# Router products of 64 columns instead of 8 in the prologue, and 64 filling matmuls instead of 32 before the first slot

## The chip, the cores and the metric

The kernel runs on one core of a Trainium2 chip. The metric is the device time of one launch in microseconds, the median of several runs; lower is better.

## What is computed

A macaron block on x of 4 batches × 1024 tokens × 128 features, all float32:

```python
x = x + 0.5 * ffn(layernorm(x))      # top-1 mixture of 8 experts, 128 -> 512 -> 128, relu
x = x + attn(layernorm(x))           # 16 heads of 8, decayed linear attention in chunks of 128
x = x + 0.5 * ffn(layernorm(x))      # the same weights again
# inside ffn
logits = xf @ Wr.T + br              # Wr is 8 x 128
expert_idx = argmax(logits, axis=-1)
h = relu(einsum('td,efd->etf', xf, W1) + b1[:, None, :])
y = einsum('etf,edf->etd', h, W2) + b2[:, None, :]
out = y[expert_idx, arange(tokens)]
```

## The kernel before

Tokens are cut into 32 tiles of 128; four of them (the same chunk of each batch) make a step, and there are 8 steps. Five engines run their own instruction streams, written out by hand, with semaphores between them.

Each FFN pass computes only the chosen expert. The tokens of a group (group 0 is steps 0 to 4, group 1 steps 5 to 7) are sorted by expert into slots of 128 rows that each belong to one expert: 27 slots for group 0 and 19 for group 1. GpSimd gathers a slot's rows (L396) from a copy of the normalised rows in DRAM. TensorE transposes them (L1208), ScalarE copies the transpose to SBUF (L545), TensorE makes the four up products (L1216, 8 instructions), ScalarE and VectorE apply bias and relu (L560 and L924), TensorE makes the down product (L1226, 8 instructions), VectorE adds the bias (L937) and the result is stored to y_d. The second half of one slot's up products waits for L924 of the slot before. TensorE issues the transpose of slot G+1 first, then up of G, then down of G-1. In the first pass a table of extra work, by turn, sits between slots on VectorE: the rest of layer norm (turns 0 to 2) and the routing of group 1 (turns 3 to 13: L780 to L791 is turn 3). GpSimd then fetches the results back (L410).

The prologue runs before the first slot. On TensorE, in this order:

- `keep_warm_by_columns(WARM0)`: matmuls whose result nobody reads, with 32 columns of weights and 128 columns streamed (L1166).
- Nine rounds. Round r transposes step r (L1170, 4 instructions), and then multiplies the transposed step r-1 by the router weights (`route_product`, L1176): 4 products, which are 8 matmul instructions with a weight load each, 8 columns streamed. After the transposes of round 3 and its product comes one product for the sum of the router weights (L1364). In round 6 `route_counts(0)` (L1183, L1184) waits for VectorE's one-hot matrix of group 0.
- The gate and bias products (L1367, L1369), and `invert(0)` (L1192), whose result is the list of tokens by slot.
- `keep_warm_by_columns(WARM1)` again, then the slots.

ScalarE copies each transposed step to SBUF (L537). VectorE takes layer-norm statistics (L702), then scales the logits once the products of steps 0 to 4 are done (L789, L791), finds the best expert and the one-hot matrix (up to L814), counts and places tokens (L820 to L873), writes the experts of the slots (L903) and, after the inversion, the list of tokens (L884, token_in) that the first gather waits for.

```python
for i in range(count):
    for c in range(0, P, 32):
        mm(bank[3][c:c + 32, 0:P], ident[:, 0:32], const_sb[:, 0:P], start=True, stop=True)
```

`const_sb` begins with the identity; `wr_sb` holds the router weights, 8 columns. The products of group 0 go to bank 4, 8 columns for each tile, 160 in all, and those of group 1 to bank 6, 96 in all.

Of the kernel before, what the change touches and what calls it, by code (L numbers as in the profile page):

```python
# [15 lines left out]
P = 128  # L16
BATCH, SEQ, D = 4, 1024, 128
STEPS = SEQ // P
TOKEN_TILES = BATCH * STEPS
EXPERTS, FF = 8, 512  # L20
# [8 lines left out]
def list_units():  # L29
    units, start = [], 0  # L30
    for layer, split in enumerate(SPLIT):
        first = 0
        for steps in split:
            tiles = steps * BATCH
            units.append(Unit(layer, first, tiles, tiles + EXPERTS - 1, start))
            first += tiles
            start += tiles + EXPERTS - 1
    return units


UNIT = list_units()
# [31 lines left out]
CONST_W = _at  # L73
# [12 lines left out]
def wait(eng, sem, value):  # L86
    if value > 0:
        eng.wait_ge(sem, value)
# [15 lines left out]
def build(nc, x, w1t, bias, w2t, wrt, br, wqkv, wg1t, wg2, wo, gamma, beta, decay, const, out):  # L104
    with ExitStack() as ctx:
        def sb(name, shape, dt=F32):
            return ctx.enter_context(nc.sbuf_tensor(name, shape, dt))

        def pb(name, shape=(P, 512)):
            return ctx.enter_context(nc.psum_tensor(name, list(shape), F32))  # L110

        def sem(name):
            return ctx.enter_context(nc.semaphore(name))
# [15 lines left out]
        hT_a, hT_b = ([sb(f"hT_{h}{i}", [P, 2 * P]) for i in range(2)] for h in "ab")  # L129

        decay_sb = sb("decay_sb", [P, HEADS * P])
        const_sb = sb("const_sb", [P, CONST_W])
        wr_sb = sb("wr_sb", [P, EXPERTS])
        br_sb = sb("br_sb", [P, EXPERTS])
        wr_sum = sb("wr_sum", [P, EXPERTS])
        wqkv_sb = sb("wqkv_sb", [P, 3 * D])
# [10 lines left out]
        rnT = [sb(f"rnT{i}", [P, BATCH * P]) for i in range(2)]  # L147
# [60 lines left out]
        bank = [pb(f"bank{i}") for i in range(8)]  # L208
# [4 lines left out]
        def cst(name, rows_=P):  # L213
            a, w = CONST[name]
            return const_sb[0:rows_, a:a + w]
# [15 lines left out]
        wr_loaded, br_loaded, wg_loaded, attn_w_loaded = sem("wr_loaded"), sem("br_loaded"), sem("wg_loaded"), sem("attn_w_loaded")  # L231
# [6 lines left out]
        wr_summed, wr_sum_copied = sem("wr_summed"), sem("wr_sum_copied")  # L238
# [30 lines left out]
        table_loaded = sem("table_loaded")  # L269
        halved, ends_known = sem("halved"), sem("ends_known")  # L270

        WARM0, WARM1 = 3, 4
        LANE_PARTS = 4
        assert SPLIT[0] == (5, 3)

# [10 lines left out]
        router_bank = [bank[4], bank[6]]  # L286
# [231 lines left out]
        @block.scalar  # L518
        def _(act):
            act.dma_start(const_sb[:, 0:EARLY_W], const[:, 0:EARLY_W]).then_inc(ident_loaded, 16)  # L520
            act.dma_start(wr_sb[:, :], wrt).then_inc(wr_loaded, 16)
            act.dma_start(br_sb[:, :], br.partition_broadcast(P)).then_inc(br_loaded, 16)

            act.wait_ge(ident_loaded, 16)
# [158 lines left out]
            for i in range(2 * SPLIT[0][1]):  # L683
                r, lo = SPLIT[0][0] + i // 2, i % 2 * 2
# [468 lines left out]
        def _(pe):  # L1153
            mm = nc.tensor.matmul
# [13 lines left out]
            def transpose4(dst, src, done):  # L1168
                for b in range(BATCH):
                    last = nc.tensor.transpose(dst[:, b * P:(b + 1) * P], src(b), ident)  # L1170
                last.then_inc(done, 1)

            def route_product(r, par, dst, at):
                pe.wait_ge(rnT_copied, r + 1)
                for b in range(BATCH):
                    last = mm(dst[:, at + b * EXPERTS:at + (b + 1) * EXPERTS], rnT[par][:, b * P:(b + 1) * P], wr_sb[:, :],  # L1176
                              start=True, stop=True)
                last.then_inc(logits_ready, 1)

            def route_counts(u):  # L1180
                pe.wait_ge(onehot_ready[u], 1)
                n = UNIT[u].tiles * EXPERTS
                mm(counts_bank[:, 0:n], upper_bf[:, :], onehot_bf[:, 0:n], start=True, stop=True)  # L1183
                mm(counts_bank[:, n:2 * n], ones_bf[:, :], onehot_bf[:, 0:n], start=True, stop=True).then_inc(counts_ready[u], 1)  # L1184
# [133 lines left out]
            def attention(k):  # L1318
                cur, nxt = step(k), step(k + 1)
                has_cur, has_nxt = 0 <= k < STEPS, 0 <= k + 1 < STEPS  # L1320
                for h in range(PAIRS):
                    if has_cur:
                        state_product(cur, h)
                    if h == 0 and 0 <= k - 2 < STEPS:
                        out_product(step(k - 2))
                    if has_nxt:
                        if h == 0 and k >= 0:
                            norm_transpose(nxt)
                        if 1 <= h <= BATCH:
                            project(nxt, h - 1)  # L1330
                        if h == BATCH + 2:
                            q_transpose(nxt)
                    if has_cur and h == BATCH + 1:
                        gate_product(cur)
                    if 0 <= k - 3 and h == BATCH + 2:
                        route_transpose(step(k - 3))
                if has_cur:
                    inter_product(cur)
                    if k + 1 < STEPS:
                        carry_product(cur)  # L1340
                if 0 <= k - 3:
                    s = step(k - 3)
                    route_product(STEPS + s.n, s.par, bank[4], 0)
                if 0 <= k - 1 < STEPS:
                    out_transpose(step(k - 1))
# [4 lines left out]
            for r in range(STEPS + 1):  # L1350

                if r < STEPS:
                    pe.wait_ge(x_loaded[r], 16)
                    wait(pe, rnT_copied, r - 1)
                    transpose4(bank[r % 2], lambda b: x_of(r * BATCH + b), rnT_ready)
                if r == SPLIT[0][0] + 1:
                    pe.wait_ge(bf_ready, 1)
                    route_counts(0)
                if r >= 1:
                    g = 0 if r - 1 < SPLIT[0][0] else 1  # L1360
                    route_product(r - 1, (r - 1) % 2, router_bank[g], (r - 1 - UNIT[g].first // BATCH) * BATCH * EXPERTS)
                if r == 3:
                    pe.wait_ge(const_loaded, 16)
                    mm(bank[7][:, 0:EXPERTS], cst("ones"), wr_sb[:, :], start=True, stop=True).then_inc(wr_summed, 1)  # L1364
            pe.wait_ge(wg_loaded, 16 * 2)
            pe.wait_ge(b1_loaded, 16)
            mm(bank[3][:, 0:D], wg1_sb, wg2_sb, start=True, stop=True)  # L1367
            for f in range(FB):
                last = nc.tensor.transpose(bank[3][:, D + f * EXPERTS:D + (f + 1) * EXPERTS], b1_rows[:, f * P:(f + 1) * P],  # L1369
                                           ident[0:EXPERTS, 0:EXPERTS])  # L1370
# [11 lines left out]
            for k in TURNS:  # L1382
                attention(k)
                if k == ROUTE_TURN:
# [3 lines left out]
                    invert(2)  # L1388
            pe.wait_ge(qS_done, STEPS * PAIRS)
            route = lambda s: route_product(STEPS + s, s % 2, bank[4], 0)  # L1390
            expert_pass(1, {
                0: lambda: out_transpose(step(7)), 1: lambda: route(5), 2: lambda: out_product(step(7)),
# [65 lines left out]
```

## Time and profile before

| | |
|---|---|
| median of 3 runs | 430.17 us (429.95 to 430.38) |
| profiled execution | 426.96 us, its span 424.9 us |
| mean granted TensorE clock | 0.909 of full |
| TensorE busy | 358.1 us, 84% of the span |
| VectorE, ScalarE, GpSimd busy | 68%, 45%, 67% |
| x to SBUF | 8 loads of 256 KB |

TensorE's clock has two levels, 2.4 GHz (1.00 in the profile) and 1.2 GHz (0.50). Times in the rows are microseconds from the span's start. A matmul's own duration includes its way through the pipeline; what a run of matmuls costs is the distance from one group to the next, which the chain of waits shows.

### The profile page before, as it was taken

To read this page: it belongs to the slowest core of one execution; us is meant where nothing else is said; L and a number is where in the kernel's file an instruction comes from. 1 tells how busy PE (TensorE), PEld (TensorE's weight loads), DVE (VectorE), ACT (ScalarE), POOL (GpSimd) and SP (SyncE) were. 2 spreads that over 40 slices of the span, in tenths; PEclk is the share of its full clock that TensorE was granted. 3 is DMA by queue.
4 is the path that set the end of the run, shared out by engine and by line. 5 is a ranking of instruction groups with operands and counts; after the bars stand their busy time and mean duration, and the time that the engine had idled before them with its cause. 6 is when DMAs were issued, how large, how long until landed. Compare 5 with 4: busy or idle time off the path is not lost.

```text
span 424.9 us, 10262 instructions
## 1 busy us (share of the span) xinstructions
PE 358.1 (84%) x2508; PEld 319.2 (75%) x2508; DVE 288.4 (68%) x995; ACT 192.1 (45%) x608; POOL 284.5 (67%) x303
## 2 busy tenths in 40 slices
PE   6788989999989979879897978855589999999920
PEld 6787879999978767667676766645489899999910
DVE  4872675444563698999898989897665676566510
ACT  5723745565546322535456363240455435555500
POOL 0027774754885999998989777620777777777770
PEclk9555999999999979998999999986599999999975
DMA  8938686887761000001010110102687846767410
GB/s 231 349 107 270 194 240 186 223 190 231 219 188 41 21 0 19 2 19 57 7 62 2 50 49 2 50 2 71 191 238 246 199 139 193 228 198 199 134 35 0
DMA packets 41303, 54.00 MB, mean 127 GB/s; under 512 B 6212, under 2 KB 25818, under 8 KB 40992
## 3 DMA queue, kind: packets, MB, share of 16 engines
q1 hardware_dynamic: 34640, 39.97, 29.9%
q0 software_dynamic: 6176, 13.26, 13.0%
q8 instruction: 23, 0.38, 0.3%
q10 hardware_dynamic: 432, 0.14, 0.2%
q14 instruction: 32, 0.26, 0.2%
HBM read 41.93 MB, written 12.32 MB: 128 GB/s over the span
## 4 chain that ended last, share of the span: by engine, by line
PE 55%; POOL 15%; DVE 11%; issue 10%; ACT 3%; DMA 2%; DVEq 1%; POOLq 0%; ACTq 0%
PE bank L1226 17%; PE bank L1216 17%; POOL outer_all L451 5%; PE bank L1272 4%; POOL rows L410 4%; PE bank L1176 4%; PE bank L1170 3%; POOL qS L459 3%; PE bank L1254 3%; PE bank L1208 2%; PE bank L1192 2%; POOL out_x L429 2%; PE bank L1290 2%; DVE st L702 1%; POOL kd L438 1%
## 5 line engine op out<-in xcount | busy, mean ns | idle before, releaser
L396 POOL DMA_INDIRECT ring<-rows_d,token_in x92 | 87.8, 955 | 78.0 <-DVE token_in L884 50.9
L1216 PE MATMUL bank<-slot_xT,w_ring 128*128 128x128 f32 x736 | 103.9, 283 | 4.9 <-DVE hT_b L924 4.0
L1216 PEld LDWEIGHTS bank<-slot_xT,w_ring 128*128 128x128 f32 x736 | 93.6, 197 | 8.6 <-DVE hT_b L924 6.0
L924 DVE TENSOR_SCALAR hT_b<-bank,b_cur 128x128 f32<-128x128 f32 x184 | 56.0, 346 | 38.2 <-PE bank L1216 32.6
L451 POOL TENSOR_TENSOR outer_all<-qkv 128x512 f32<-128x512 f32 x64 | 66.4, 1063 | 4.0 <-ACT qkv L577 4.0
L1272 PE MATMUL bank<-outer_all,decay_sb 128*128 128x256 f32 x256 | 68.0, 392 | 1.0 <-DVE qS L966 1.0
L560 ACT ACTIVATE hT_a<-bank,b_cur 128x128 f32<-128x128 f32 x184 | 57.3, 363 | 12.4 <-PE bank L1216 11.5
L1226 PE MATMUL bank<-w_sb,hT_a 128*128 x368 | 59.2, 284 | 3.4 <-DVE ring L937 0.6
L1272 PEld LDWEIGHTS bank<-outer_all,decay_sb 128*128 128x128 f32 x256 | 48.3, 197 | 16.6 <-issue 5.4
L1226 PE MATMUL bank<-w_sb,hT_b 128*128 x368 | 56.5, 276 | 0.0
L429 POOL DMA_INDIRECT out_x<-ring,token_out x46 | 46.1, 1002 | 14.0 <-issue 11.9
L1226 PEld LDWEIGHTS bank<-w_sb,hT_a 128*128 128x128 f32 x368 | 48.8, 193 | 7.9 <-issue 7.5
L553 ACT ACTIVATE b_cur<-b_t 128x4 f32 x92 | 18.8, 205 | 70.4 <-DVE hT_b L924 58.8
L1226 PEld LDWEIGHTS bank<-w_sb,hT_b 128*128 128x128 f32 x368 | 48.9, 194 | 0.0
L459 POOL TENSOR_TENSOR qS<-qS 128x256 f32<-128x256 f32 x49 | 35.6, 729 | 18.5 <-DVE qS L966 18.3
L975 DVE TENSOR_REDUCE o_in<-qS 128x64 f32<-128x256 f32 x64 | 44.2, 700 | 2.4 <-POOL qS L459 2.4
L966 DVE TENSOR_TENSOR qS<-bank,qkv 128x512 f32<-128x512 f32 x64 | 43.3, 683 | 3.7 <-PE bank L1272 3.6
L410 POOL DMA_INDIRECT rows<-y_d,slot_of x32 | 30.5, 955 | 15.4 <-DMA y_d<-kd 8.2
L545 ACT ACTIVATE slot_xT<-bank 128x128 f32<-128x128 f32 x92 | 25.0, 271 | 24.2 <-PE bank L1208 21.0
L1208 PE MATMUL bank<-const_sb,ring 128*128 128x128 f32 x92 | 26.3, 286 | 7.9 <-issue 5.0
L916 DVE TENSOR_TENSOR ring<-ring,b_sb 128x128 f32<-128x128 f32 x46 | 13.5, 294 | 21.6 <-issue 17.6
L1254 PE MATMUL bank<-wqkv_sb,xnT 128*128 128x384 f32 x64 | 26.2, 496 | 1.2 <-ACT xnT L582 1.2
(127 smaller groups left out, 498.8 us busy)
## 6 DMA issues: line engine op xcount, KB each, us to landing
w_ring<-in_w1t SPq DMA_DIRECT2D x92, 256.0 KB
rows_d<-rows SPq DMA_DIRECT2D x8, 512.0 KB, 2.9
y_d<-kd SPq DMA_DIRECT2D x46, 64.0 KB
rows<-in_x SPq DMA_DIRECT2D x8, 256.0 KB, 5.9
w_sb<-in_w2t SPq DMA_DIRECT2D x1, 2048.0 KB, 8.8
rows_d<-rows SPq DMA_DIRECT2D x8, 256.0 KB, 3.7
ring<-rows_d,token_in POOLq DMA_INDIRECT x92, 4.0
decay_sb<-in_decay SPq DMA_DIRECT2D x1, 1024.0 KB, 8.1
```

The costliest lines, as they stand in the source:

```text
L396: pool.indirect_dma_start(n_in_ring(G) if layer_of(G) == 0 else in_ring(G), None, rows_d[u], bass.IndirectOffsetOnAxis(ap=token_in[u][:, j ...
L410: pool.indirect_dma_start(n_of(t), None, y_d[u], bass.IndirectOffsetOnAxis(ap=slot_of[u][:, t - UNIT[u].first:t - UNIT[u].first + 1], axis ...
L429: pool.indirect_dma_start(out, bass.IndirectOffsetOnAxis(ap=token_out[u - GROUPS][:, at:at + 1], axis=0), x_in_ring(G), None, bounds_check ...
L451: pool.tensor_tensor(outer[n % 2][:, h * PW:(h + 1) * PW].rearrange("p (a d e) -> p a d e", d=HD, e=HD), k_, v_, ALU.mult).then_inc(outer_ ...
L459: pool.tensor_tensor(v[:, :, 0], v[:, :, 0], v[:, :, 1], ALU.add).then_inc(halved, 1)
L560: last = nc.scalar.activation(hT_a[G % 2][:, f * P:(f + 1) * P], bank_a[:, f * P:(f + 1) * P], ACT.Relu, bias=b1_cur[G % 2][:, f:f + 1])
L924: last = nc.vector.tensor_scalar(hT_b[G % 2][:, f * P:(f + 1) * P], bank_b[:, f * P:(f + 1) * P], b1_cur[G % 2][:, 2 + f:3 + f], 0.0, ALU. ...
L966: nc.vector.tensor_tensor(qS[h % 4][:, :].rearrange("p (b a e) -> p b a e", b=BATCH, e=HD), bank[h % 3][:, :].rearrange("p (b a e) -> p b ...
L975: nc.vector.tensor_reduce(o_in[:, h * w:(h + 1) * w].rearrange("p (a e) -> p a e", e=HD), qS[h % 4][:, :].rearrange("p (a d e) -> p a e d" ...
L1216: last = mm(to[:, f * P:(f + 1) * P], w1_ring[G % W1_BUFS][:, (2 * half + f) * P:(2 * half + f + 1) * P], slot_xT[G % 2][:, :], start=True ...
L1226: last = mm(y_bank[l][:, 0:D], h[:, f % 2 * P:(f % 2 + 1) * P], w2_sb[:, bass.ds(expert[G] + f * D, D)], start=(f == 0), stop=(f == FB - 1))
L1272: last = mm(to, decay_sb[:, (2 * h + a) * P:(2 * h + a + 1) * P], outer[s.par][:, h * PW + a * w:h * PW + (a + 1) * w].rearrange("p (b w) ...
```

## The change

The router weights and the constants, which begin with the identity, become one tile, so that a product of 64 columns can stream the 8 router columns and the first 56 columns of the identity behind them. `route_product` takes a width; the eight calls of the prologue give 64. Each of the four products of a step now writes 64 columns of its bank from its own place on; of these the last 56 are written over by the next products, or lie beyond what is read. The calls in the later passes keep 8 columns. WARM1 goes from 4 to 8, which is 64 filling matmul instructions instead of 32.

```diff
-        const_sb = sb("const_sb", [P, CONST_W])
-        wr_sb = sb("wr_sb", [P, EXPERTS])
+        wr_const = sb("wr_const", [P, EXPERTS + CONST_W])
+        wr_sb, const_sb = wr_const[:, 0:EXPERTS], wr_const[:, EXPERTS:EXPERTS + CONST_W]
...
-        WARM0, WARM1 = 3, 4
+        WARM0, WARM1, WIDE = 3, 8, 64
...
-            def route_product(r, par, dst, at):
+            def route_product(r, par, dst, at, width=EXPERTS):
+
                 pe.wait_ge(rnT_copied, r + 1)
                 for b in range(BATCH):
-                    last = mm(dst[:, at + b * EXPERTS:at + (b + 1) * EXPERTS], rnT[par][:, b * P:(b + 1) * P], wr_sb[:, :],
-                              start=True, stop=True)
+                    last = mm(dst[:, at + b * EXPERTS:at + b * EXPERTS + width], rnT[par][:, b * P:(b + 1) * P],
+                              wr_const[:, 0:width], start=True, stop=True)
                 last.then_inc(logits_ready, 1)
...
-                    route_product(r - 1, (r - 1) % 2, router_bank[g], (r - 1 - UNIT[g].first // BATCH) * BATCH * EXPERTS)
+                    route_product(r - 1, (r - 1) % 2, router_bank[g], (r - 1 - UNIT[g].first // BATCH) * BATCH * EXPERTS,
+                                  WIDE)
```

## Rows read from the trace of the kernel before

**Rows 1.** The page: granted clock in 40 slices, and the chain by engine.

```profile
PEclk9555999999999979998999999986599999999975
...
PE 55%; POOL 15%; DVE 11%; issue 10%; ACT 3%; DMA 2%; DVEq 1%; POOLq 0%; ACTq 0%
```

**Rows 2.** Stretches: length, busy of PE, PEld, DVE, ACT, POOL, clock, DMA share, GB/s.

```profile
9.00:10.00 1.00, 1.00 (x11) 1.00 (x10) 0.97 (x6) 0.94 (x2) 0.00 (x0) 0.89 1.10 325
33.00:40.00 7.00, 6.09 (x24) 5.17 (x25) 1.82 (x8) 2.34 (x10) 5.17 (x7) 0.50 0.90 277
40.00:41.00 1.00, 1.00 (x9) 1.00 (x8) 0.10 (x1) 0.23 (x2) 0.70 (x2) 0.75 0.78 258
60.00:100.00 40.00, 39.24 (x348) 38.65 (x348) 21.52 (x78) 21.58 (x80) 20.47 (x22) 1.00 0.77 209
155.00:159.00 4.00, 4.00 (x15) 3.44 (x15) 3.90 (x13) 0.40 (x1) 3.61 (x4) 0.50 0.00 0
```

**Rows 3.** TensorE in order of time: start, duration, line, count, wait.

```profile
4.92 1.78 PE L1170 MATMUL bank<-const_sb,rows 128*128 128x128 f32 x8
...
28.61 1.94 PE L1166 MATMUL bank<-const_sb 128*32 128x128 f32 x32
33.01 0.47 PE L1208 MATMUL bank<-const_sb,ring 128*128 128x128 f32 x1 [2.47 <-DMA ring<-rows_d,token_in]
...
43.43 0.71 PE L1216 MATMUL bank<-slot_xT,w_ring 128*128 128x128 f32 x4 [0.23 <-DVE hT_b L924]
```

**Rows 4.** The chain of waits in order of time: start, duration, what.

```profile
8.28 0.79 PE bank L1176 x8
9.07 0.49 PE bank L1170 x4
...
13.63 0.95 PE bank L1170 x4
14.58 1.52 PE bank L1176 x8
...
36.60 0.45 PE bank L1208
...
46.09 0.71 PE bank L1216 x4
...
77.45 0.89 PE bank L1216 x8
78.34 0.89 PE bank L1226 x8
...
98.79 1.51 DMA y_d<-kd
...
156.00 1.71 PE bank L1272 x4
...
160.83 0.86 PE bank L1272 x4
```

**Rows 5.** VectorE in order of time.

```profile
14.26 0.87 DVE L702 BATCH_NORM_STATS2 st<-rows 128x6 f32<-128x128 f32 x4
16.12 0.33 DVE L789 TENSOR_TENSOR logits<-bank,rstd 128x160 f32<-128x160 f32 x1 [0.99 <-PE bank L1176]
...
28.93 0.19 DVE L884 SCALAR_TENSOR_TENSOR token_in<-bank,token_f 128x27 int32<-128x27 f32 x1
...
40.90 0.29 DVE L937 SCALAR_TENSOR_TENSOR kd<-bank,b_sb 128x128 f32<-128x128 f32 x1 [1.09 <-PE bank L1226]
```

**Rows 6.** L1176's weight loads, GpSimd's gather of slot 3, gathers to landing, 15 to 45.

```profile
L1176 PEld LDWEIGHTS bank<-wr_sb,rnT x64: 186/333/337, 6.7 to 25.0; 128*128 128x128 f32 x64
...
33.50 0.95 POOL L396 DMA_INDIRECT ring<-rows_d,token_in  x1 [0.30 <-issue]
...
ring<-rows_d,token_in POOLq DMA_INDIRECT x13, 6.5
```

More of the change, by code:

```diff
@@ L520, in _ @@
             act.dma_start(const_sb[:, 0:EARLY_W], const[:, 0:EARLY_W]).then_inc(ident_loaded, 16)
-            act.dma_start(wr_sb[:, :], wrt).then_inc(wr_loaded, 16)
+            act.dma_start(wr_sb, wrt).then_inc(wr_loaded, 16)
             act.dma_start(br_sb[:, :], br.partition_broadcast(P)).then_inc(br_loaded, 16)
@@ L1360, in _ @@
                     g = 0 if r - 1 < SPLIT[0][0] else 1
-                    route_product(r - 1, (r - 1) % 2, router_bank[g], (r - 1 - UNIT[g].first // BATCH) * BATCH * EXPERTS)
+                    route_product(r - 1, (r - 1) % 2, router_bank[g], (r - 1 - UNIT[g].first // BATCH) * BATCH * EXPERTS,
+                                  WIDE)
                 if r == 3:
                     pe.wait_ge(const_loaded, 16)
-                    mm(bank[7][:, 0:EXPERTS], cst("ones"), wr_sb[:, :], start=True, stop=True).then_inc(wr_summed, 1)
+                    mm(bank[7][:, 0:EXPERTS], cst("ones"), wr_sb, start=True, stop=True).then_inc(wr_summed, 1)
             pe.wait_ge(wg_loaded, 16 * 2)
```

## The prediction

> **What bounds the kernel now.** I read the page first [rows 1]. The chain that ended last runs through TensorE for 55% and GpSimd for 15%. The line of the granted clock is the second thing to see: it stands at half in the second, third and most of the fourth slice, which is just where the diff works. Next, stretches of that part [rows 2]: the clock falls inside 9 to 10 us and comes back inside 40 to 41. TensorE is wholly busy when it falls; half of what it does then is router products of 8 columns. It does not rise over the filling matmuls at 28.61 [rows 3], nor in the wait for gathered rows behind them; it rises at the end of 33 to 40, after its first stretch there without a gap. (The page shows the full clock before 9.8 us too, but 8 transposes at 4.92 take 1.78 us [rows 3], twice what they take later, so I take the clock as low until about 6.4.)
>
> Third, TensorE in order of time and the chain of waits [rows 3, 4], and VectorE beside them [rows 5]. VectorE stands idle for 0.99 us before L789, released by the router products L1176. From there its routing chain runs nearly without a gap to token_in at 28.93 us, which releases the first gather, whose rows reach TensorE at 33.01. Then come the slots, until the y store at 98.79, and GpSimd's fetches behind it. From 60 to 100 us TensorE works 39.24 of 40, so what the first slots give is not absorbed before that store. GpSimd's own gathers come every 1.25 us (0.95 and 0.30 of issue [rows 6]) against 1.9 us for a slot, and are no bound later.
>
> **The wide products.** 64 matmuls (8 groups of 8) now write 64 columns. Before, at the low clock, such a group with 8 columns takes 1.52 us, 0.19 each; 4 transposes with 128 columns take 0.95, 0.24 each. At the full clock it is 0.79 us a group (0.10 each) against 0.49 for 4 transposes (0.12 each) [rows 4]. The weight load alone takes a median of 333 ns there [rows 6], so it is the load that sets the pace, and columns lie behind it. 64 lie between 8 and 128 columns: a group costs 0 to 0.4 us more at the low clock and 0 to 0.2 at the full one. I take 0.05, near the lower end, as even 120 columns more add only 0.05 and 0.02 each; in the main case 2 us of slack hide all five groups ahead of L789.
>
> The Trainium skill (TensorE: Matmul & The Clock Gate, Part 1, "Wait — 56ns, not 53.3ns?") has matmuls start N ÷ 1.2 GHz apart at the low clock. By that rule 56 more columns would cost 47 ns an instruction, 3 us over 64 of them; the trace does not agree, since with 8 columns they already stand 0.19 us apart.
>
> What I expect of the width: TensorE streams more columns in the same time, and the clock that fell at 9.8 us stays up. The rows don't prove that columns count. What speaks for it is that the clock fell with the engine 100% busy, in a stretch that differs from the always-full 60 to 100 us in its thin products [rows 2].
>
> From 9.4 us (the transposes of 9.07 over) at full-clock prices: products to 10.2, L1364 to 10.4, transposes 10.9, products 11.7, transposes 12.2, products 13.0, transposes 13.5. Loads of x are not late: L702 at 14.26 waited for none [rows 5]. VectorE is free for L789 at 14.26 + 0.87 = 15.13, not 16.12: **0.99 us saved**, with 2 us of margin on TensorE's side; VectorE binds then, so it can't be more. TensorE then waits from 13.5 to about 18.2 for the one-hot, and I let the clock fall there. The counts, the last three products, L1367 and the inversion cost what they cost before, and end 0.99 earlier: inversion at 27.6, first gather at 28.42, its rows at 32.0.
>
> **The filling matmuls.** WARM1 from 4 to 8 makes 64 of them in place of 32: 1.94 us at 28.61 [rows 3] becomes some 3.6 us at the low clock, 27.6 to 31.3. They lie beside the gather, whose rows come at 32.0, and cost nothing; with that cover gone, up to 1.7 us. The nearest case for what they do to the clock is the start: 24 of them and the transposes of 4.92 stand before the rise at 6.4, while 32 at 28.61 raised nothing. 64 on top of the inversion is more than either, so I expect the rise at 30 to 31 us. It may fall again in the waits for rows up to 34.
>
> **The first slots.** At the full clock a slot is 0.89 us up, 0.89 down [rows 4], 0.11 transpose. Slot 0: transpose 32.0, up 32.65 to 33.5. Slot 2's rows were there by 36.60 [rows 4], so by 35.6 now; up of slot 1 to 36.5, down of slot 0 to 37.4. Slot 3's gather is issued at 33.50 and such a gather takes 6.5 us there [rows 6]: 40.0 before, 39.0 now. Up of slot 2 is 39.1 to 40.0, down of slot 1 to 40.9, up of slot 3 from 41.0, 42.60 before. Here a second gain comes in. Before, the down of slot 0 ended only at 40.9 (L937 waited 1.09 us for it [rows 5]), VectorE's layer-norm steps of turn 2 came behind it, and L924 behind these, for which TensorE waited until 43.43 [rows 3]; a slot later again, until 46.09 [rows 4]. Now these steps run while TensorE waits for rows. VectorE's turn 3 (L780 to L791, 1.2 us) ends at 42.4, L924 for slot 3 at 43.4, and the second half of slot 4's up starts at about 43.5 in place of 46.09: 2.6 us in all, 1.6 beyond the 0.99. With the clock low through slots 1 and 2 (rise at 40.5 as before) the same count gives 44.1, 2.0 us in all. From there both kernels have the full clock. I take **1.4 us** for this part, of 1.0 to 1.6.
>
> **Sum:** 0.99 + 1.4 = 2.4 us. The profiled execution took 426.96 us (its span 424.9), the runs 430.17; taken off the median, 427.8 us.
>
> **Rivals.**
> A. The clock is kept in the prologue, but the fill does not raise it before slot 0, or not for long: 0.99 plus 0 to 0.4, as gathers bind slots 2 and 3: 428.9.
> B. The products do not keep it, the fill raises it: L789 waits as before, or longer by 5 × 0.2; the slots give 1.0 to 1.6: 428.6 to 430.2.
> C. The timed runs are 3.2 us above the profiled one. If they never get the clock at 6.4 us, L789 stands later in them. A round costs 1.52 + 0.95 at the low clock and 0.79 + 0.49 at the full one, so the two or so rounds between 6.4 and 9.8 us come 2.1 us later, all of it removed as VectorE binds at 15.13. Gain 4.5: 425.7. For it is the gap; against it, a profiled execution may differ in fixed parts.
> D. Slower: the clock falls at another place of attention. It already stands low from 155 to 159 [rows 2], and a shift of all work by 2.4 us moves the stalls that make it fall. One more stretch of 3.4 us of dense matmuls costs up to 1.7 us (4 of L1272 take 1.71 at 156.00 and 0.86 at 160.83 [rows 4]). From two such on it outweighs the gain: 430.17 - 2.4 + 3.4 = 431.2. Against it: the same shift can spare the first of them.
> E. Neither half acts on the clock: 430.2, up to 1.0 more for wide products.
> F. The page's spacing rule holds as a price per column: by the upper bound from rows, the five groups ahead of L789 cost 0.4 each, 2.0 us, at a low clock: 432.2. Against it are the spacings above.
>
> **Chances:** forecast 0.42, A 0.15, B 0.09, C 0.14, D 0.08, E 0.10, F 0.02. The likeliest case's own range is 427.0 to 428.5. Over the cases it is 425.5 (C) to 430.4 (E), which leaves out D, F and the far end of C. A change of 0.2% (0.86 us) is about what a measurement here can tell. Faster: the forecast, C, A but for a little, most of B: 0.78. Same: E, parts of A, B and D: 0.13. Slower: 0.09.
>
> **What the profile would show.** The clock at full past 9.8 us to 13 or later, with 8 products still 0.8 us; L789 at about 15.1 with no wait for L1176; L884 at about 27.9; the clock back before 33 us; the first slot's transpose at 32.0; TensorE's waits for L924 at 43 and 46 gone. I am wrong if the clock falls at 9.8 again, if 64 columns stretch the groups, if rows land no earlier, or if new low stretches stand in attention.

## The result, and the profile after

The changed kernel takes 426.35 us (median of 22 runs, 424.70 to 432.19), the kernel before 429.91 us (22 runs beside them, 427.03 to 431.63). The ratio is 0.9934, with a 95% interval of 0.9909 to 0.9958: faster by 0.4 to 0.9%. (It is worked out from the runs; the ratio of the two medians is 0.9917.) A second measurement of the same two kernels, at the end of the study, gave 428.41 against 429.88 us and a ratio of 0.9973 (0.9933 to 1.0013). That interval includes no change at all, so the size of the gain is not well known. The profiled execution took 424.76 us (span 423.0), where the one of before took 426.96 (424.9). It is the second fastest of the 22, and that of before is faster than all 22 beside it.

In this measurement both kernels have two groups of executions with a gap between them. Of the 22 before, 16 lie above 429.3 us and the rest at 427.0 to 427.7; of the changed kernel's 22, 5 lie above 429 and 17 at 424.7 to 427.3. (The second measurement of the changed kernel, 425.8 to 431.3, fills the gap.) The profiled execution of each kernel is from its lower group. So the change did two things: it made the lower group faster, and it moved most executions into it. The prediction had the first as its forecast and the second as rival C.

The page of the changed kernel, clock and chain, against [rows 1]:

```profile
PEclk9858999999999969999999999975599999999975
...
PE 45%; POOL 21%; DVE 13%; issue 12%; DMA 3%; ACT 2%; DVEq 1%; POOLq 0%; SPq 0%; ACTq 0%
```

The second and the fourth slice, at half before, are at 0.8 now, the third still at 0.5. TensorE's share of the chain is down from 55 to 45%. Stretches of the changed kernel, columns as in [rows 2]:

```profile
9.00:10.00 1.00, 1.00 (x12) 1.00 (x11) 0.97 (x6) 0.94 (x2) 0.00 (x0) 1.00 1.10 315
10.00:13.00 3.00, 3.00 (x31) 3.00 (x29) 2.59 (x18) 1.19 (x2) 0.00 (x0) 1.00 1.22 371
18.00:28.00 10.00, 9.94 (x68) 9.63 (x72) 7.76 (x29) 5.02 (x14) 0.00 (x0) 0.50 0.48 141
31.00:34.00 3.00, 1.74 (x14) 1.25 (x10) 0.08 (x1) 0.48 (x2) 2.24 (x3) 0.92 0.92 272
35.00:38.00 3.00, 2.81 (x13) 2.81 (x14) 0.78 (x4) 1.11 (x4) 2.39 (x3) 0.50 0.94 323
```

The clock no longer falls inside 9 to 10 us; it is full to beyond 13, low from the wait for the one-hot on, back for slot 0 (0.92 over 31 to 34), and low once more for slot 1. TensorE in order of time, the changed kernel, against [rows 3]. Its lines are one or two further down: L1177 is the router product, L1209, L1217 and L1227 a slot's transpose, up and down, L1193 the inversion.

```profile
8.52 1.00 PE L1177 MATMUL bank<-wr_const,rnT 128*128 128x64 f32 x8
9.36 0.61 PE L1170 MATMUL bank<-wr_const,rows 128*128 128x128 f32 x4
...
27.49 3.64 PE L1166 MATMUL bank<-wr_const 128*32 128x128 f32 x64
32.02 0.33 PE L1209 MATMUL bank<-wr_const,ring 128*128 128x128 f32 x1 [0.90 <-DMA ring<-rows_d,token_in]
32.72 1.16 PE L1217 MATMUL bank<-slot_xT,w_ring 128*128 128x128 f32 x8 [0.37 <-ACT slot_xT L545]
...
35.46 1.92 PE L1217 MATMUL bank<-slot_xT,w_ring 128*128 128x128 f32 x8
```

A group of 8 wide products costs 0.84 us (8.52 to 9.36) against 0.79 for narrow ones. The filling matmuls end at 31.1, 0.9 us before the rows of slot 0, and the clock rises just after them, at about 31.5. Up of slot 0 is at the full clock, 1.16 us; that of slot 1 at the low one, 1.92. VectorE, the changed kernel, against [rows 5]:

```profile
14.15 0.87 DVE L702 BATCH_NORM_STATS2 st<-rows 128x6 f32<-128x128 f32 x4
14.94 0.31 DVE L789 TENSOR_TENSOR logits<-bank,rstd 128x160 f32<-128x160 f32 x1
...
27.82 0.19 DVE L884 SCALAR_TENSOR_TENSOR token_in<-bank,token_f 128x27 int32<-128x27 f32 x1
...
38.92 0.29 DVE L937 SCALAR_TENSOR_TENSOR kd<-bank,b_sb 128x128 f32<-128x128 f32 x1 [0.89 <-PE bank L1227]
...
43.45 0.61 DVE L924 TENSOR_SCALAR hT_b<-bank,b_cur 128x128 f32<-128x128 f32 x2 [0.77 <-DVE logits L791]
```

L789 follows L702 without a wait, 1.18 us earlier than before; token_in is 1.11 earlier, L937 after slot 0 1.98. That difference stays: the store of slot 26, the last one that GpSimd's first fetch (L410) needs, goes out at 95.02 instead of 96.90, the fetch begins at 98.37 instead of 100.30, and the span is 1.9 us shorter.

A second profile of the same kernel, from the second measurement (426.24 us, span 424.4), shows how far one profile can be trusted. TensorE in order of time:

```profile
27.98 3.07 PE L1166 MATMUL bank<-wr_const 128*32 128x128 f32 x64
32.58 0.33 PE L1209 MATMUL bank<-wr_const,ring 128*128 128x128 f32 x1 [1.53 <-DMA ring<-rows_d,token_in]
33.28 1.68 PE L1217 MATMUL bank<-slot_xT,w_ring 128*128 128x128 f32 x8 [0.37 <-ACT slot_xT L545]
```

The clock rises and falls in the same places, but about 1.2 us earlier against the work: it is up from about 6.4 to 16.7 and from 30.3 to 33.7 us, where the first profile has 7.6 to 17.8 and 31.5 to 34.9. So it falls before the up of slot 0 is done, and that takes 1.68 us and not 1.16. L789 again waits for nothing, but it starts at 15.42, since VectorE gets there later; L937 after slot 0 is 0.86 earlier than before, and the span is only 0.5 shorter. The changed kernel's two profiles give 1.9 and 0.5 us.

### The profile page after: what moved, and what is told of

It reads as the page before. It is cut to its first block, busy times and chain, and to the rows that moved or that the text cites. A ratio compares the mean times of both kernels' runs of the same rounds, so it can differ in the third digit from the quotient of the medians.

```text
span 423.0 us, 10326 instructions
## 1 busy us (share of the span) xinstructions
PE 355.9 (84%) x2540; PEld 316.9 (75%) x2540; DVE 288.1 (68%) x995; ACT 192.8 (46%) x608; POOL 285.5 (68%) x303
## 3 DMA queue, kind: packets, MB, share of 16 engines
q1 hardware_dynamic: 34640, 39.97, 30.3%
## 4 chain that ended last, share of the span: by engine, by line
PE 45%; POOL 21%; DVE 13%; issue 12%; DMA 3%; ACT 2%; DVEq 1%; POOLq 0%; SPq 0%; ACTq 0%
PE bank L1227 16%; PE bank L1217 15%; POOL outer_all L451 8%; POOL rows L410 5%; POOL qS L459 3%; PE bank L1273 3%; PE bank L1177 2%; POOL out_x L429 2%; DVE st L702 2%; PE bank L1255 2%; PE bank L1209 2%; PE bank L1193 2%; PE bank L1170 1%; DMA rows<-in_x 1%; PE bank L1291 1%
## 5 line engine op out<-in xcount | busy, mean ns | idle before, releaser
L396 POOL DMA_INDIRECT ring<-rows_d,token_in x92 | 88.8, 965 | 75.3 <-DVE token_in L884 48.2
L1217 PE MATMUL bank<-slot_xT,w_ring 128*128 128x128 f32 x736 | 102.6, 281 | 4.3 <-DVE hT_b L924 3.5
L1217 PEld LDWEIGHTS bank<-slot_xT,w_ring 128*128 128x128 f32 x736 | 92.7, 196 | 7.3 <-DVE hT_b L924 5.0
L924 DVE TENSOR_SCALAR hT_b<-bank,b_cur 128x128 f32<-128x128 f32 x184 | 55.9, 345 | 37.4 <-PE bank L1217 31.8
L1227 PE MATMUL bank<-w_sb,hT_a 128*128 x368 | 59.8, 285 | 4.5 <-issue 1.6
L1227 PE MATMUL bank<-w_sb,hT_b 128*128 x368 | 56.3, 276 | 0.0
L1227 PEld LDWEIGHTS bank<-w_sb,hT_a 128*128 128x128 f32 x368 | 48.7, 193 | 9.1 <-issue 8.6
L429 POOL DMA_INDIRECT out_x<-ring,token_out x46 | 46.1, 1001 | 14.0 <-issue 11.6
L1227 PEld LDWEIGHTS bank<-w_sb,hT_b 128*128 128x128 f32 x368 | 48.7, 193 | 0.0
L410 POOL DMA_INDIRECT rows<-y_d,slot_of x32 | 30.6, 955 | 15.3 <-DMA y_d<-kd 8.1
L1209 PE MATMUL bank<-wr_const,ring 128*128 128x128 f32 x92 | 26.1, 284 | 6.7 <-issue 4.7
```

The lines of the kernel that those rows point to most:

```text
L396: pool.indirect_dma_start(n_in_ring(G) if layer_of(G) == 0 else in_ring(G), None, rows_d[u], bass.IndirectOffsetOnAxis(ap=token_in[u][:, j ...
L410: pool.indirect_dma_start(n_of(t), None, y_d[u], bass.IndirectOffsetOnAxis(ap=slot_of[u][:, t - UNIT[u].first:t - UNIT[u].first + 1], axis ...
L429: pool.indirect_dma_start(out, bass.IndirectOffsetOnAxis(ap=token_out[u - GROUPS][:, at:at + 1], axis=0), x_in_ring(G), None, bounds_check ...
L924: last = nc.vector.tensor_scalar(hT_b[G % 2][:, f * P:(f + 1) * P], bank_b[:, f * P:(f + 1) * P], b1_cur[G % 2][:, 2 + f:3 + f], 0.0, ALU. ...
L1217: last = mm(to[:, f * P:(f + 1) * P], w1_ring[G % W1_BUFS][:, (2 * half + f) * P:(2 * half + f + 1) * P], slot_xT[G % 2][:, :], start=True ...
L1227: last = mm(y_bank[l][:, 0:D], h[:, f % 2 * P:(f % 2 + 1) * P], w2_sb[:, bass.ds(expert[G] + f * D, D)], start=(f == 0), stop=(f == FB - 1))
```

## The experiments

All were timed beside the kernel before. Upper group means runs above 429 us. With 8 columns that is a clean cut (the kernel before has no run between 428.4 and 429.3 in 126); with more columns it is a rough one, and with 256 all runs lie above it because the kernel is slower.

| kernel | columns | last fill | runs | upper group | median us | ratio to before |
|---|---|---|---|---|---|---|
| before, four measurements | 8 | 32 | 126 | 75 | 429.63 to 429.91 | 1 |
| changed | 64 | 64 | 22 | 5 | 426.35 | 0.9934 (0.9909 to 0.9958) |
| changed, again | 64 | 64 | 12 | 5 | 428.41 | 0.9973 (0.9933 to 1.0013) |
| wide only | 64 | 32 | 12 | 1 | 427.63 | 0.9971 (0.9942 to 0.9999) |
| fill only | 8 | 64 | 12 | 5 | 427.34 | 0.9969 (0.9937 to 1.0001) |
| width 32 | 32 | 64 | 12 | 3 | 427.13 | 0.9948 (0.9912 to 0.9983) |
| early fill, narrow | 8 | 32 | 12 | 2 | 427.58 | 0.9984 (0.9955 to 1.0012) |
| early fill, wide | 64 | 64 | 12 | 1 | 427.37 | 0.9961 (0.9932 to 0.9990) |
| both waits filled | 64 | 64 | 12 | 8 | 431.84 | 1.0021 (0.9974 to 1.0069) |
| fill of 128 | 64 | 128 | 12 | 4 | 427.61 | 0.9979 (0.9940 to 1.0018) |
| width 128 | 128 | 64 | 12 | 0 | 426.21 | 0.9940 (0.9906 to 0.9974) |
| width 128, fill of 96 | 128 | 96 | 12 | 1 | 426.81 | 0.9912 (0.9875 to 0.9948) |
| width 128, one wait filled | 128 | 64 | 12 | 0 | 426.81 | 0.9924 (0.9891 to 0.9956) |
| width 256 | 256 | 64 | 10 | 10 | 431.87 | 1.0053 (1.0008 to 1.0098) |

### Each half alone

The changed kernel with the old fill:

```diff
-        WARM0, WARM1, WIDE = 3, 8, 64
+        WARM0, WARM1, WIDE = 3, 4, 64
```

> Theory (columns streamed keep the clock up; each half has its own gain): with 64 columns but the old fill of 32, the clock rises at about 6.4 to 9 us and stays at full until TensorE waits for the one-hot; L789 starts at about 15.0 without a wait for the router products, and everything up to the first gather is 1.0 to 1.2 us earlier than before. The fill raises nothing, slot 0 runs at the low clock, so the slots give 0 to 0.4 more: 1.0 to 1.6 us below the kernel before, 1 us above the changed kernel. Rival (it is the fill that does it, the width only costs): L789 at 16.1 or later, and no gain.

In its profiled execution the prologue does what was expected: L789 at 15.23, the first gather at 28.58 instead of 29.41, 0.83 earlier. Its slots:

```profile
33.30 2.07 PE L1217 MATMUL bank<-slot_xT,w_ring 128*128 128x128 f32 x8 [0.37 <-ACT slot_xT L545]
...
36.56 2.05 PE L1217 MATMUL bank<-slot_xT,w_ring 128*128 128x128 f32 x8
```

Both ups take what they took before. The head start of 0.83 us at the gather is 0.56 when the rows of slot 0 are there (32.45 against 33.01), 0.45 at L937 after slot 0 (40.45) and 0.28 at the first fetch L410 (100.02). So the gather's landing took the first part of it. For the rest, the clock came back at 40.7 us, at 40.5 before: slots at the low clock that begin earlier still wait for the full clock until the same moment. I had put this case at 0.99 to 1.4 us; the profile gives 0.4 of span. In the median it still gains 2.0 us, since only 1 of 12 runs is in the upper group. Its ratio, 0.9971, is hardly clear of 1. So the width acts mostly on the share of the groups, and within the lower group (median 427.59 of 11) it alone gives nothing against some 427.3 before.

The fill alone:

```diff
-        WARM0, WARM1, WIDE = 3, 8, 64
+        WARM0, WARM1, WIDE = 3, 8, 8
```

> Theory: with 8 columns and the fill of 64, the clock falls again at most 3.4 us after it rose, L789 stands at 16.1 or later (up to 18 where the clock never rises), the first gather at 29.4 or later. The fill raises the clock at about 31 us and slot 0 runs at the full clock: up of slot 0 in 0.9 to 1.2 us and not 1.9. Gain 0.9 us against the kernel before, less than the changed kernel by 1.1. Rival (the width only costs): as fast as the changed kernel, or faster.

Its profiled execution (430.20 us) is one of the upper group, and shows what that group is. TensorE in order of time:

```profile
6.80 1.88 PE L1177 MATMUL bank<-wr_const,rnT 128*128 128x8 f32 x8
8.53 1.09 PE L1170 MATMUL bank<-wr_const,rows 128*128 128x128 f32 x4
...
36.76 1.16 PE L1217 MATMUL bank<-slot_xT,w_ring 128*128 128x128 f32 x8 [0.37 <-ACT slot_xT L545]
...
39.84 1.91 PE L1217 MATMUL bank<-slot_xT,w_ring 128*128 128x128 f32 x8
```

and VectorE:

```profile
18.96 0.32 DVE L789 TENSOR_TENSOR logits<-bank,rstd 128x160 f32<-128x160 f32 x1 [2.81 <-PE bank L1177]
```

Every group of the prologue is at the low price, 1.73 us for the one at 6.80; L789 waits 2.81 us and starts at 18.96, 2.84 later than in [rows 5]. The clock is first at full just behind the fill, at about 35.7 us. The page shows a full clock before that, as nothing is recorded until the first change; the spacings decide. For the same reason such an execution shows a higher mean clock than one in which the clock did rise early. In the three measurements of the kernel before that list it for each run, 57 of the 59 runs above 429 have a mean clock of 0.938 or more, and all 45 below have 0.905 to 0.914. The fill does its own part here, up of slot 0 in 1.16 us. Its upper group stands at 430.1 (median) against 430.8 of the kernel before beside it, its lower one at 427.2 against 427.4, so alone it gives 0.2 to 0.7 us, less than the 0.9 expected; its ratio, 0.9969, is not clear of 1.

### Columns as the cause

Width 32:

```diff
-        WARM0, WARM1, WIDE = 3, 8, 64
+        WARM0, WARM1, WIDE = 3, 8, 32
```

> Width 32 instead of 64, fill 64. Theory (columns count, by degree): a group of 8 products costs the same as with 64, 0.79 to 0.85 us at the full clock; whether the clock holds past 9.8 us is open, since the columns streamed lie half way between the two kernels; if it holds, L789 at 15.0 and the time of the changed kernel within 0.3 us, if it falls, L789 between 15.3 and 16.2. Rival (any wider product will do, the tile's new place is what counts): as the changed kernel.

Three of 12 runs are in the upper group, the profiled one (430.02 us) among them; a group there takes 1.57 us. Eight others lie at 424.9 to 427.3, where the changed kernel's lower group is, and one at 428.84 shows the mean clock of the upper one (0.941). Between the widths 32 and 64 these numbers can't tell.

Early filling matmuls on a tile of zeros, from 1.3 us on, with 8 columns and the old last fill (WARM0, WARM1, WIDE = 3, 4, 8), and then with the changed kernel's columns and fill:

```diff
+        WARM_E = 5
...
+            pe.wait_ge(carry_done, 1)
+            for i in range(WARM_E):
+                for c in range(0, P, 32):
+                    mm(bank[2][c:c + 32, 0:P], carry[:, 0:32], carry[:, 0:P], start=True, stop=True)
             pe.wait_ge(ident_loaded, 16)
             keep_warm_by_columns(WARM0)
```

> The kernel before (8 columns, fill of 32) plus 40 filling matmuls on a tile of zeros from about 1.3 us on, before the identity has landed (so far TensorE begins at 3.5). Theory (the runs at 429.4 us and above are those in which the clock never rises in the prologue, since what TensorE streams from 3.5 to 6.7 us doesn't suffice at every start; and 8 columns can't hold it): the clock rises in every run at 4 to 8 us, the runs above 429.4 vanish (18 of 35 so far), the profile shows it fall again about 3.4 us after the rise; L789 at 16.1 to 16.6; median 427.5. Rival (the two groups of runs come from something else, or matmuls of zeros don't count): half of the runs stay above 429.4.

The narrow kernel with an early fill, TensorE in order of time:

```profile
1.32 2.36 PE L1352 MATMUL bank<-carry 128*32 128x128 f32 x40 [1.32 <-POOL carry L381]
...
7.64 0.96 PE L1178 MATMUL bank<-wr_const,rnT 128*128 128x8 f32 x8
...
12.42 1.71 PE L1178 MATMUL bank<-wr_const,rnT 128*128 128x8 f32 x8
```

and its stretches:

```profile
9.00:11.00 2.00, 1.87 (x19) 1.78 (x18) 1.83 (x12) 0.73 (x3) 0.00 (x0) 1.00 1.19 308
12.00:14.00 2.00, 2.00 (x12) 2.00 (x11) 1.83 (x13) 1.13 (x3) 0.00 (x0) 0.50 0.93 379
```

The clock rises at 4.7 us, and with 8 columns falls again at 11.6, in the middle of the products. TensorE is busy there but for a gap of 0.13 us before 10.02, and such a gap is not what does it: the changed kernel's second profile has one of 0.24 at 10.67, and there the clock holds to 16.7. None of the 12 runs has the mean clock (0.938 and more) of an execution without an early rise, where 19 of 35 of the kernel before have it; two lie at 429.69 for another reason that stays open (0.897 and 0.904). The median falls by 2.1 us to 427.58, close to the lower group of before (427.2 to 427.4), though the ratio, 0.9984, is not clear of 1. That shows what the upper group of the kernel before is: the executions in which the clock doesn't rise in the prologue.

One expectation failed. The wait at L789 (L790 here) is gone, 1.36 us earlier than before and not at 16.1 or later:

```profile
14.76 0.30 DVE L790 TENSOR_TENSOR logits<-bank,rstd 128x160 f32<-128x160 f32 x1
```

Yet the median is no lower than the lower group of before, and the span of the profile is 0.5 us shorter. A head start of the prologue alone, with slots 0 and 1 at the low clock, is worth little here.

> The changed kernel (64 columns, fill of 64) with the same 40 early matmuls on zeros. Theory: the clock rises in every run by 8 us and holds until the wait for the one-hot, so the changed kernel's slow group (5 of 22 runs at 429 or more) vanishes; median 425.5 (424.5 to 427.3), 1 us below the changed kernel. No gain within the fast group, since L789 waits for VectorE at 15.0 already. Rival: a part of the runs stays at 429 or more.

One of 12 is above 429, as expected, but the median is 427.37 and not 425.5. Its profile shows why a sure rise isn't all: the clock rose at 5.2, held to 15.5, and was next up at 39.4. The fill from 27.45 to 31.1 raised nothing here, and slots 0 and 1 ran low:

```profile
27.45 3.64 PE L1167 MATMUL bank<-wr_const 128*32 128x128 f32 x64
...
33.02 2.07 PE L1218 MATMUL bank<-slot_xT,w_ring 128*128 128x128 f32 x8 [0.37 <-ACT slot_xT L546]
```

The same 64 matmuls raised the clock in the changed kernel's profile. So the gain from a full clock in slot 0 is there in some executions and not in others. That an early fill moves executions into the lower group mostly without this gain would explain the median, but it is argued from one profile.

Widths 128 and 256:

```diff
-        WARM0, WARM1, WIDE = 3, 8, 64
+        WARM0, WARM1, WIDE = 3, 8, 128
```

> The changed kernel with 128 columns instead of 64. Theory (the more columns stream, the surer the clock rises early, the price of a column being hidden behind the weight load): a group of 8 takes 0.85 to 0.9 us at the full clock and 1.7 at the low one, as with 64; the clock rises early in as many runs or more, median 426 or less. Rival (columns are paid): groups 0.1 us or more longer, and with VectorE binding at L789 still no more than 0.3 us slower.

```profile
8.21 1.06 PE L1177 MATMUL bank<-wr_const,rnT 128*128 128x128 f32 x8
9.11 0.60 PE L1170 MATMUL bank<-wr_const,rows 128*128 128x128 f32 x4
```

A group takes 0.90 us, 0.06 more than with 64 columns, and no run is in the upper group. Over all kernels without an early fill (and without the one that fills both waits, with 8 of 12), 80 of 138 runs with 8 columns lie above 429, 15 of 58 with 64, and 1 of 36 with 128 (on the chip of the latter, 9 of 24 with 64). That is the clearest sign that the columns act on how often the clock rises early.

> 256 columns. Theory (columns are free only up to what a weight load covers, 0.11 us an instruction at the full clock): a matmul of 256 columns takes 0.22 us, a group of 8 about 1.75 at the full clock in place of 0.9, and twice that at the low one. The products of steps 0 to 4 then end at 16.5 to 17.5, and TensorE again releases L789, 1.5 to 2.5 us later than in the changed kernel; the inversion starts later too: 2 to 4 us slower than the changed kernel. Rival (the group's price doesn't depend on columns at all): as with 128.

The kernel with 256 columns, TensorE, then VectorE:

```profile
8.97 1.89 PE L1177 MATMUL bank<-wr_const,rnT 128*128 128x256 f32 x8
10.70 0.60 PE L1170 MATMUL bank<-wr_const,rows 128*128 128x128 f32 x4
```

```profile
17.57 0.33 DVE L789 TENSOR_TENSOR logits<-bank,rstd 128x160 f32<-128x160 f32 x1 [1.75 <-PE bank L1177]
```

A group takes 1.73 us. From 8 to 128 columns it grew by 0.11 us, from 128 to 256 by 0.83: up to 128 the columns lie nearly free behind what sets the pace with 8, and somewhere beyond it they are paid. TensorE releases L789 again, at 17.57, and the kernel is 5 us slower than the one with 128, though in its profile the clock rises early (6.8 us) and holds to 20.5.

### Filling the waits

Two more fills, on a bank that nobody reads:

```diff
+        WARM_A, WARM_B = 16, 12
...
                 if r == SPLIT[0][0] + 1:
+                    keep_warm_by_columns(WARM_A, bank[2])
                     pe.wait_ge(bf_ready, 1)
                     route_counts(0)
...
+            keep_warm_by_columns(WARM_B, bank[2])
             invert(0)
```

> The changed kernel with two more fills, into a bank that nobody reads: 128 matmuls while TensorE waits for the one-hot (3.4 us at the full clock, of a wait of 4.0), and 96 before the inversion. Theory (the clock falls in that stall and makes the last three products and the inversion slow): with the stall filled the clock stays at full from 7 to 31 us; the products of steps 5 to 7 and L1193 take half, the inversion waits for VectorE instead of TensorE: ends about 24.9 + 1.6 in place of 27.5, first gather 0.7 to 1.0 us earlier than in the changed kernel, and with the clock still up through slots 0 and 1 another 0 to 0.5: 0.7 to 1.5 us faster than it. Rival (where the clock isn't up in time, the fills at the low clock take 6.8 us and push the counts out): a part of the runs is 2 to 3 us slower.

The kernel with both waits filled, TensorE in order of time and one stretch:

```profile
14.15 3.69 PE L1167 MATMUL bank<-wr_const 128*32 128x128 f32 x126
...
20.31 2.23 PE L1178 MATMUL bank<-wr_const,rnT 128*128 128x64 f32 x16
...
25.84 2.24 PE L1194 MATMUL bank<-outer_all 128*128 128x54 bf16 x20
```

```profile
25.90:28.00 2.10, 2.10 (x22) 1.94 (x20) 0.75 (x5) 0.21 (x1) 0.00 (x0) 1.00 0.00 0
```

The clock held from 7.0 to 34.3 us and the last 16 product instructions fell from 3.5 to 2.2 us. But the inversion took 2.24 us at the full clock, and takes 2.24 in the changed kernel at the low one, so what I expected of it isn't there. It also begins later than in the changed kernel (25.84 against 25.32), behind 2.8 us of fill, so even with the clock up nothing is won. Eight of 12 runs are above 429, most at 432: the rival. That these are the executions without an early rise, in which the fill lasts twice as long, fits their time but was not seen in a profile; and why there should be 8 of 12, where the changed kernel has 10 of 34 with the same work in front of the fill, is open.

Half the first fill, with 128 columns and nothing before the inversion:

```diff
-        WARM0, WARM1, WIDE = 3, 8, 64
+        WARM0, WARM1, WIDE = 3, 8, 128
+        WARM_A, WARM_B = 8, 0
```

> 128 columns, fill of 64 as in the changed kernel, and 64 filling matmuls in the wait for the one-hot (1.7 us at the full clock, of a wait of 4; a fill of 128 there went wrong). Theory: the clock holds through the wait in most runs, the last three products take half, the inversion waits for VectorE and begins 0.2 to 0.4 earlier; it takes 2.2 us at either clock, as seen. Gain 0 to 0.4 against the kernel with 128 columns. Rival (each filling matmul there is instruction traffic that delays the counts): 0.5 to 1 slower.

```profile
24.98 2.25 PE L1194 MATMUL bank<-outer_all 128*128 128x54 bf16 x20 [2.17 <-DVE outer_all L874]
27.16 3.64 PE L1167 MATMUL bank<-wr_const 128*32 128x128 f32 x64
```

The inversion now waits 2.17 us for VectorE, which shows what is next in line: with the clock up in the wait, TensorE has nothing more to give before it. All 12 runs lie within 425.62 to 427.30. Its ratio (0.9924) is not clear of that of width 128 alone (0.9940).

### The length of the last fill

```diff
-        WARM0, WARM1, WIDE = 3, 8, 64
+        WARM0, WARM1, WIDE = 3, 16, 64
```

> The changed kernel with WARM1 at 16, 128 filling matmuls. Theory: 64 take 3.6 us from 27.5 and end 0.9 us before the rows of slot 0; of the 64 more, at least half run at the full clock, so the fill ends at 32.5 to 34 and slot 0 begins 0.5 to 2 us late. In return the clock is still up at 35 us, where slot 1 runs, and not low from 34.9 to 38.3. TensorE waits for slot 2's rows until 35.2 in any case, so the delay of slot 0 costs little: between 0.8 us faster and 0.5 slower than the changed kernel. Rival (no cover left, so what is added is paid in full): 1.5 us slower.

The kernel with a fill of 128, TensorE in order of time:

```profile
27.34 5.40 PE L1166 MATMUL bank<-wr_const 128*32 128x128 f32 x128
32.68 0.33 PE L1209 MATMUL bank<-wr_const,ring 128*128 128x128 f32 x1
...
35.64 1.13 PE L1217 MATMUL bank<-slot_xT,w_ring 128*128 128x128 f32 x8 [0.22 <-ACT hT_a L560]
```

Slot 0 begins 0.66 us later than in the changed kernel, but slot 1 runs at the full clock, and L937 after slot 0 is at 37.82, 1.1 us earlier. At 98 us this is lost again. The store of slot 26 in the changed kernel, then here, and GpSimd's first fetch here:

```profile
95.02 0.32 SPq L354 DMA_DIRECT2D y_d<-kd  x1
```

```profile
94.11 0.32 SPq L354 DMA_DIRECT2D y_d<-kd  x1
...
98.48 0.94 POOL L410 DMA_INDIRECT rows<-y_d,slot_of  x1 [9.26 <-DMA y_d<-kd]
```

The store goes out 0.9 us earlier than in the changed kernel, but the fetch begins 4.4 us after it and not 3.35, at 98.48 against 98.37. And from there to the end it takes 326.4 us, where the changed kernel takes 324.6. The same two losses stand in other profiles (times in us; all are executions with an early rise; the second column tells the clock in the up of slots 0 and 1, the third when the transpose of slot 0 starts):

| profile | slots 0, 1 | rows of slot 0 | store of slot 26 | L410 | span |
|---|---|---|---|---|---|
| before | low, low | 33.01 | 96.90 | 100.30 | 424.9 |
| wide only | low, low | 32.45 | 96.60 | 100.02 | 424.5 |
| early fill, narrow | low, low | 31.68 | 95.90 | 99.55 | 424.4 |
| early fill, wide | low, low | 32.18 | 95.94 | 100.57 | 424.6 |
| changed | full, low | 32.02 | 95.02 | 98.37 | 423.0 |
| changed, again | part, low | 32.58 | 96.25 | 99.72 | 424.4 |
| width 128 | full, low | 32.00 | 95.59 | 99.06 | 424.4 |
| fill of 128 | full, full | 32.68 | 94.11 | 98.48 | 424.9 |
| width 128, fill of 96 | full, full | 33.04 | 94.36 | 99.22 | 425.4 |

Up to the store the clock in the slots decides: at full in both, it comes 2.5 to 2.8 us earlier than before, although the rows came 0.3 us earlier or no earlier at all. Behind the store that gain is lost: the fetch follows it after 3.3 to 4.9 us, and the rest takes 324.1 to 326.4 us. The longer rests go with low stretches of attention at other places (with a fill of 128 also at 208 to 212 and 246 to 249 us), but not in every profile, so their cause is open. Differences of a microsecond between two profiles can come from this alone.

> 128 columns and WARM1 at 12, 96 filling matmuls. Theory: no run stays low in the prologue; the fill takes 27.4 to about 32, ends as the rows of slot 0 land, and the clock is up for slot 0 in every run and more often for slot 1: 0 to 0.6 us below the kernel with 128 columns and 64 filling matmuls. Rival (what counts is where the rise falls, and a longer fill only delays slot 0): same or 0.5 slower.

With 128 columns and 96 filling matmuls the median is 426.81, that of width 128 in another measurement 426.21; 424.00 is the lowest time of the study. The ratio, 0.9912, is the best, but its interval overlaps those of its neighbours, so a gain of the longer fill is not shown.

> The changed kernel once more, beside the three others. Theory: two groups of runs again, most (about 17 of 22 so far) at 424.7 to 427.3 us, where the clock rises before 9 us, the rest at 429 or more; median 426 to 427. Rival (128 columns aren't better than 64, the two medians of 426.35 and 426.21 are one): within 0.3 us of the kernel with 128 columns.

Five of 12 in the upper group: with 10 of 34 the changed kernel's share is nearer a third than the 5 of 22 first seen (8 of the ten show a mean clock of 0.935 or more, two do not). And only 4 of 12 lie at 424.7 to 427.3, where I expected most. Beside it, on the same chip, both kernels with 128 columns that ran there were faster (0.9924 and 0.9912 against 0.9973, with intervals that overlap). So 128 columns are likely a better version than the change, by some 1 us in the mean over all runs (426.6 against 427.5); the intervals don't settle it.

## Why the prediction was right, and where it was off

- **The width keeps the clock: right.** The full clock held past 9.8 us (to 17.8), groups of 8 took 0.84 us, and L789 lost its wait. Forecast 0.99 us earlier, measured 1.18, of which 0.11 is L702 itself standing earlier; in the second profile it is 0.70. The clock fell in the wait for the one-hot, as I let it. Cause shown: in both profiles with 8 columns and an early rise it fell in the middle of the products (9.8 and 11.6 us), in all ten with 64 or more not before 15.5, when the products of group 0 and the transposes behind them were done. The tile's new place is not the cause, since the narrow early fill has it too.
- **The price of the columns: right.** 0.05 us a group forecast, 0.05 measured (0.79 to 0.84) at the full clock, and 0.03 at the low one (a group behind the counts, 1.65 to 1.68). A price per column, rival F, did not show at 64 columns; it showed between 128 and 256. One reading behind it was off: the load's median of 333 ns is that of the low clock, at the full one it is 192, and both are longer than the distance between two products (0.19 and 0.10 us). So the length of a load did not prove that loads set the pace; the spacings did the work.
- **The fill: right in this profile.** 27.6 to 31.3 forecast, 27.5 to 31.1 measured; hidden by the gather; slot 0 at the full clock, and the fall before slot 1 that I allowed. But in the second profile the clock fell again within slot 0's up, and in another execution (wide early fill) the same fill raised nothing, so it is no sure thing.
- **The slots: the size was off.** I took 1.4 us beyond the prologue; measured, the store of slot 26 is 1.88 us earlier, of which 1.1 is the prologue, so 0.8. Slot 1 ran at the low clock, nearer the lower variant of my count (2.0 us in all; L937 shows 1.98 and L924 at 43.45 against 45.43 also 1.98). The fill of 128 shows the other variant: with slots 0 and 1 both at the full clock the store comes 2.79 us earlier. Together the profile shows 1.9 of span, for 2.4 forecast; the second profile of the same kernel shows 0.5. The waits for L924 at 43 and 46 us are not gone but moved: TensorE waits for it 0.9 us in all between 40 and 60 us, 0.8 before.
- **The store I named was the wrong one.** I ended the slots at the store at 98.79, as the profile's chain does. By the program L410 needs the stores of slots 23 to 26, and slot 26's is the one at 96.90; the store at 98.79 is already group 1's. The forecast doesn't hang on it, as both move by 1.88 us, but the 1.51 us behind it is no landing time that counts: from the right store to L410 it is 3.4 us.
- **Rival C was no rival but a second gain, and I gave it 0.14.** The 3.2 us between the profiled execution and the median before were not a fixed part; the profile was drawn from the lower group. The low-clock prologue costs 2.84 us at L789 (18.96 with the fill alone, 16.12 before), I had computed 2.1 for two rounds. Fewer executions of that kind are the larger half of the gain in the mean: means fell by 2.6 us (429.54 to 426.94), and 11 of 22 runs fewer in a group that is 2.8 to 3.5 us slower is some 1.6 us of it.
- **Rival A was mis-sized**: 0.99 to 1.4 expected, 0.4 in the profile. A head start of the prologue is not kept in full: it lost 0.27 us before the rows landed and more in slots that wait for the same rise.
- **D** was not seen as a loss here. The low stretch of attention is at 151 to 158 us now, in place of 153 to 160, moved with the work; at 281 to 305 the clock is low throughout, where before it was up for 3.4 us in between; and from L410 to the end both take 324.6 us. In other kernels that part took up to 1.8 us more.

The median, 426.35, came out below the forecast of 427.8 by 1.45 us and outside the 427.0 to 428.5 of the likeliest case; only the range over all cases holds it. Two misses of opposite sign make that up: 0.5 too much taken for the slots, by the first profile, and the rest, some 2 us, for the executions moved, of which the forecast had none. That they partly cancel is luck, and so is it that the second measurement's 428.41 falls within the likeliest case's range.

## What to carry to other kernels

Where TensorE works with thin products, each with its own weight load, more columns can be streamed for next to nothing, and that is a way to hold its full clock: in this kernel, in float32, a group of 8 products cost 0.79 us with 8 columns, 0.84 with 64, 0.90 with 128, and 1.73 with 256. Look at the spread of the times before reading one profile: where runs fall into two groups, the profile shows one of them, and a change can act on how often each occurs. Filling matmuls are only worth it under cover that lasts in the slow case: a fill that fits the wait at the full clock takes twice as long without it (64 of them 1.95 us and 3.64). And a microsecond won early is not won at the end until it is seen there: of 2.8 us at the store of slot 26, a fill of 128 kept 1.8 at the next step and none in the span.

## What was not expected of the hardware

- The clock's first rise came at different moments with the same work in front: 6.4 to 7.6 us in the profiles whose first 3 us of matmuls were the same, and in two others (8 and 32 columns) not before 35.7 and 43.0 us. The changed kernel itself, profiled twice, had 7.6 and 6.4. What sets the moment stays open; no run tested it.
- Matmuls on zeros count towards the clock's rise: with 40 of them in front it came at 4.7 and 5.2 us, and none of 24 runs has the mean clock of an execution without it.
- The inversion's 20 bf16 matmuls of 54 columns take 2.24 us at either clock, 0.11 each, while a slot's up takes 1.9 to 2.1 us at the low clock and 1.1 to 1.2 at the full one.
- A profile's clock before the first recorded change reads 1.00 even where each matmul shows the low one.
- From the store of slot 26 to the fetch that waits for it, it took from 3.3 to 4.9 us at the same place of the program.
